# Attention probabilities: two f16 parts turned by one transposing DMA per head, in place of four TensorE transposes

## The chip, the cores and the metric

The kernel runs on one core of one Trainium2 chip. The metric is the device time of one execution in microseconds; lower is better. TensorE (PE), VectorE (DVE), ScalarE (ACT), GpSimd (POOL) and SyncE (SP) each run their own instruction list in order and meet only at semaphores. DMAs are issued by SP here, all on one queue. SBUF and PSUM are the two on-chip memories; TensorE writes only to PSUM.

## What is computed

Two layers over `x` of 32 x 64 x 256: cross-attention and a mixture of experts, then a second attention and a grouped feed-forward. Only the first attention is touched:

```python
q = _proj_heads(input_q, Wq, bq)          # 32 batches, 8 heads, 256 x 8 each
k = _proj_heads(input_k, Wk, bk)
v = _proj_heads(input_v, Wv, bv)
scores = jnp.einsum('bhnd,bhmd->bhnm', q, k) / math.sqrt(D_HEAD)
scores = scores + key_masks[:, None, :, :]
attn = jax.nn.softmax(scores, axis=-1)
out = jnp.einsum('bhnm,bhmd->bhnd', attn, v)
```

For each of 32 x 8 = 256 pairs of batch and head there is a 256 x 256 matrix of probabilities, which must be transposed before it multiplies V, since TensorE contracts over partitions.

## The kernel before

The program is a software pipeline written out by hand. Every engine runs the loop `for n in steps: step(n)`; a step holds eight half steps `i = 0..7`, and half step `g = 8 * n + i` of steps 0 to 31 is batch `n`, head `i`. There are 256 of these. The order of the calls inside `step` is the order on the engine; no scheduler changes it.

For a half step g the chain over the engines is: TensorE `scores(g)` (two matmuls of 256 columns into the PSUM bank `ps1`, shown as `ps` in the profile); VectorE `maxima(g)` (adds the mask, takes the row's extreme into `low_max`, once for each half of the rows); ScalarE `exps(g)` (into `p32`, f32 in SBUF, shown as `p`); TensorE `turn_p(g)` (four 128 x 128 f32 transposes into the PSUM bank `psT`); ScalarE `p_high(g)` (the f16 high part `p_hi`, scaled by 4096); VectorE `p_low(g)` (the f16 rest `p_lo`); TensorE `times_v(g)` (eight matmuls of 25 columns into `psV`). `scores(g)` waits for `exps(g - 1)`, since there is one score bank. Once per step VectorE takes `psV` out with `pv_out`, the only place that runs line 1075.

Three other streams are woven into the same half steps:

- Steps 0 to 7: weights of one expert per step are loaded by SP in three stages of 512 KB, turned by TensorE, copied by ScalarE and split in f16 parts by GpSimd (`w_parts`, lines 486 and 488).
- Steps 5 to 36: 128 units of the experts, one for each two half steps. TensorE `unit_gate` (even half), `unit_up` (odd half), `unit_down` (both); ScalarE `unit_tanh` and `unit_high`; VectorE `gate_mul` (odd half), `up_mul` (even half), `add_expert`; GpSimd `h_low` (line 493).
- For each pair of steps: projections, `cut_qk` and `cut_v` on GpSimd, layer norms and the router (`attention_to_x`, `norm2`, `route_keep`) on VectorE. SP stores the split q and k to DRAM (`store_parts`) and loads them again in stacked form (`load_stacks`, 12 DMAs).

Steps 35 to 43 hold the second layer, which the change does not edit.

## Time and profile before

| | |
|---|---|
| runs | 1111.68, 1112.45, 1113.06 us, median 1112.45 |
| profiled execution | 1112.29 us, of which the span is 1110.4 us |
| PE busy | 921.4 us (83%) |
| DVE busy | 846.0 us (76%) |
| ACT busy | 581.6 us (52%) |
| POOL busy | 364.3 us (33%) |
| DMA queue q1 | 53.93 MB, 16.2% of 16 engines |

The span runs from the first to the last instruction. Busy time is the union of an engine's instructions; instructions of one engine overlap a little, so the start of one and the start of the next say more about its pace than its duration. The 256 half steps lie between about 41 and 867 us.

### The profile page before, as it was taken

What the parts mean: (1) busy time and instruction counts of PE and PEld (TensorE: products, weight loads), DVE (VectorE), ACT (ScalarE), POOL (GpSimd) and SP (SyncE); (2) the same over time, 40 slices, a digit from 0 to 9 for tenths busy, and PEclk for the clock granted to TensorE, in tenths of its full rate; (3) what the DMA queues carried; (4) which work ended last, traced back from release to release, by engine and by line L of the source; (5) the groups of instructions that cost most, each with busy time, mean ns of one, the idle gap of its engine ahead of it and who ended that gap; (6) DMA issues with size and microseconds to landing.
All of it is one profiled execution on the core that took longest, in us unless ns stands there. A gap on an engine that the chain in (4) does not pass through costs nothing.

```text
span 1110.4 us, 26634 instructions
## 1 busy us (share of the span) xinstructions
PE 921.4 (83%) x10039; PEld 813.5 (73%) x10039; DVE 846.0 (76%) x2442; ACT 581.6 (52%) x1258; POOL 364.3 (33%) x410
## 2 busy tenths in 40 slices
PE   2465658889999999999999999999999979866564
PEld 1355547878888888888888888888888857755454
DVE  2556757787989889898989898898988676565552
ACT  1355555566666666666666666666666313322221
POOL 5456454644142322323232323322312322221111
PEclk9867678999999999999999999999999989887877
DMA  4623232302020202111020202011000040001000
GB/s 135 174 68 119 67 119 68 120 31 63 11 63 11 72 2 73 32 43 55 19 63 12 63 12 72 25 44 44 26 12 1 1 143 11 2 25 35 20 30 19
DMA packets 49186, 55.62 MB, mean 50 GB/s; under 512 B 4380, under 2 KB 42276, under 8 KB 49060
## 3 DMA queue, kind: packets, MB, share of 16 engines
q1 hardware_dynamic: 49060, 53.93, 16.2%
q8 instruction: 80, 1.31, 0.5%
q14 instruction: 46, 0.38, 0.1%
HBM read 45.53 MB, written 8.39 MB: 49 GB/s over the span
## 4 chain that ended last, share of the span: by engine, by line
PE 49%; DVE 19%; issue 12%; ACT 10%; POOL 6%; DMA 1%; SPq 1%; DVEq 0%; POOLq 0%; ACTq 0%
PE psG L699 10%; PE psY L699 8%; PE psT L769 8%; PE psU L699 7%; PE ps L699 6%; PE psV L699 4%; ACT p L581 4%; DVE th_ga_h L1143 3%; ACT p_hi L589 2%; DVE ps L1057 2%; PE psM L699 2%; DVE x_res L1162 2%; PE psV L870 1%; POOL hp_lo L493 1%; DVE gt L1132 1%
## 5 line engine op out<-in xcount | busy, mean ns | idle before, releaser
L493 POOL TENSOR_TENSOR hp_lo<-th_ga_h,hp_hi 128x512 f16<-128x512 f32 x128 | 149.5, 1168 | 498.4 <-ACT hp_hi L614 498.4
L1057 DVE CUSTOM_DVE_ANT_0 ps<-ps,mask_in 128x256 f32<-128x256 f32 x512 | 207.3, 446 | 80.0 <-PE ps L699 77.0
L589 ACT ACTIVATE p_hi<-psT 128x512 f16<-128x512 f32 x256 | 152.6, 596 | 213.9 <-PE psT L769 212.5
L581 ACT ACTIVATE p<-ps,low_max 128x256 f32<-128x256 f32 x512 | 214.5, 472 | 77.4 <-DVE low_max L1057 77.3
L1066 DVE SCALAR_TENSOR_TENSOR p_lo<-psT,p_hi 128x512 f16<-128x512 f32 x256 | 176.3, 689 | 36.4 <-ACT p_hi L589 31.2
L699 PE MATMUL psU<-xT,w_gu 128*128 128x256 f16 x1536 | 189.6, 273 | 16.7 <-DVE th_ga_h L1151 10.9
L699 PE MATMUL psG<-xT,w_gu 128*128 128x256 f16 x1536 | 190.6, 274 | 5.4 <-issue 3.5
L699 PE MATMUL psY<-w_dn,hp_hi 128*128 128x256 f16 x1024 | 183.8, 275 | 0.2 <-POOL hp_lo L493 0.2
L699 PEld LDWEIGHTS psU<-xT,w_gu 128*128 128x128 f16 x1536 | 141.7, 98 | 35.3 <-DVE th_ga_h L1151 12.9
L769 PE MATMUL psT<-ident,p 128*128 128x128 f32 x1024 | 164.8, 287 | 0.0
L699 PEld LDWEIGHTS psG<-xT,w_gu 128*128 128x128 f16 x1536 | 142.8, 98 | 22.4 <-issue 6.1
L699 PE MATMUL ps<-k_stack,q_stack 128*128 128x256 bf16 x512 | 104.0, 287 | 62.4 <-ACT p L581 52.7
L699 PE MATMUL psY<-w_dn,hp_lo 128*128 128x256 f16 x512 | 140.7, 275 | 0.0
L769 PEld LDWEIGHTS psT<-ident,p 128*128 128x128 f32 x1024 | 129.6, 149 | 4.2
L699 PEld LDWEIGHTS psY<-w_dn,hp_hi 128*128 128x128 f16 x1024 | 100.9, 99 | 12.6 <-POOL hp_lo L493 0.3
L608 ACT ACTIVATE th_ga_h<-psG 128x512 f32<-128x512 f32 x128 | 76.5, 598 | 61.9 <-PE psG L699 59.3
L699 PEld LDWEIGHTS ps<-k_stack,q_stack 128*128 128x128 bf16 x512 | 42.3, 99 | 83.5 <-ACT p L581 63.1
L1143 DVE SCALAR_TENSOR_TENSOR th_ga_h<-th_ga_h,psG 128x512 f32<-128x512 f32 x128 | 86.7, 677 | 11.7 <-ACT th_ga_h L608 11.3
L699 PEld LDWEIGHTS psV<-v_parts,p_hi 128*128 128x128 f16 x1024 | 77.0, 99 | 21.5 <-issue 17.7
L1151 DVE SCALAR_TENSOR_TENSOR th_ga_h<-psU,th_ga_h 128x512 f32<-128x512 f32 x128 | 86.9, 679 | 3.8 <-PE psU L699 3.8
L699 PE MATMUL psV<-v_parts,p_hi 128*128 128x25 bf16 x1024 | 78.8, 176 | 12.7 <-DVE o_rec L1077 12.7
L614 ACT ACTIVATE hp_hi<-th_ga_h 128x512 f16<-128x512 f32 x128 | 81.0, 633 | 11.9 <-DVE th_ga_h L1151 11.9
(153 smaller groups left out, 1255.8 us busy)
## 6 DMA issues: line engine op xcount, KB each, us to landing
mask_in<-in_mask_Bx2048x_ff SPq DMA_DIRECT2D x32, 256.0 KB, 3.3
part_scratch<-parts SPq DMA_DIRECT2D x16, 384.0 KB, 3.0
q_stack<-part_scratch SPq DMA_DIRECT2D x64, 96.0 KB
k_stack<-part_scratch SPq DMA_DIRECT2D x64, 96.0 KB
stage<-in_L_ffn_gate_w SPq DMA_DIRECT2D x8, 512.0 KB, 4.4
stage<-in_L_ffn_up_w SPq DMA_DIRECT2D x8, 512.0 KB, 5.0
stage<-in_L_ffn_down_w SPq DMA_DIRECT2D x8, 512.0 KB, 4.2
ctx_in<-in_ctx SPq DMA_DIRECT2D x16, 128.0 KB, 3.1
```

Source lines behind the costliest of these rows:

```text
L493: pool.tensor_tensor(hp_lo[:, u % 2, :], hb32[:, u % 2, :], hp_hi[:, u % 2, :], ALU.subtract).then_inc(s["h_split"], 1)
L581: act.activation(p32[:, g % 2, nt, :], ps1[:, nt, :], ACT.Exp, bias=low_max[:, col:col + 1], scale=-1.0).then_inc(s["exp_done"], 1)
L589: act.activation(p_hi[:, g % 2, :, :], psT[:, :].rearrange("p (m n) -> p m n", m=2), ACT.Copy, scale=P_SCALE).then_inc(s["phi_done"], 1)
L608: act.activation(th, psG[:, :], ACT.Tanh, scale=0.5 * G_UNSCALE).then_inc(s["tanh_done"], 1)
L614: act.activation(hp_hi[:, u % 2, :], hb32[:, u % 2, :], ACT.Copy).then_inc(s["h_hi"], 1)
L699: return pe.matmul(out_, lhsT, rhs, start=start, stop=stop, skip_group_check=shares_bank)
L769: last = pe.transpose(psT[:, at:at + P], p32[:, g % 2, nt, mt * P:mt * P + P], ident[:, :])
L1057: dve.tensor_tensor_reduce(out=ps1[:, nt, :], in0=ps1[:, nt, :], in1=mask_in[:, n % 2, nt, :], scale=-1.0, scalar=HIGH, op0=ALU.add, op1=A ...
L1066: dve.scalar_tensor_tensor(out=p_lo[:, g % 2, :, :], in0=psT[:, :].rearrange("p (m n) -> p m n", m=2), scalar=P_SCALE, in1=p_hi[:, g % 2, ...
L1143: dve.scalar_tensor_tensor(out=ga, in0=th, scalar=1.0, in1=psG[:, :], op0=ALU.add, op1=ALU.mult).then_inc(s["gate_used"], 1)
L1151: dve.scalar_tensor_tensor(out=hb32[:, u % 2, :], in0=psU[:, :], scalar=0.5 * G_UNSCALE * G_UNSCALE, in1=ga, op0=ALU.mult, op1=ALU.mult).t ...
L1162: dve.scalar_tensor_tensor(out=x_res[:, row, :], in0=psY[:, eg % 2, t * D:t * D + D], scalar=tokw[:, row * NE + e:row * NE + e + 1], in1=x ...
```

## The change

`turn_p` goes, and with it 1024 TensorE transposes. ScalarE's `p_high` and VectorE's `p_low` now read the exponentials from `p32` in SBUF, before they are turned, and write the two parts side by side into `p_parts`, which has three slots. SP then issues one transposing DMA for each half step (`turn`), from `p_parts` to `p_turn`, 128 rows of 1024 f16 values, that is eight squares of 128 x 128. `times_v` reads `p_turn` and runs one half step later. The factor 4096 moves into the exponent: VectorE adds log 4096 to the two maxima in a new instruction of its own, after `maxima`, and `exps` waits for it. The bank `psT`, now free, becomes the second score bank, so `scores(g)` waits for `exps(g - 2)`.

The units of the experts start two half steps later (`unit_at`), the layer norm and router pieces move by two half steps, `add_expert` stands behind the gate and up products, `pv_out` moves from i = 1 to i = 3, and the two halves of `cut_qk` move one place later, the second one into the next even step. On SP the loads are spread over the half steps between the transposes. `LOW_ON_POOL = 8 * B` is 256, so `p_low` of every half step runs on VectorE and the GpSimd form is never issued.

```diff
+LOW_ON_POOL = 8 * B
-P_SCALE = 4096.0
+LOG_P_SCALE = math.log(4096.0)
...
+        exp_bias = eb("exp_bias", [P, 2, 2], F32)
         p32 = eb("p32", [P, 2, 2, 256], F32)
-        p_hi = eb("p_hi", [P, 2, 2, 256], F16)
-        p_lo = eb("p_lo", [P, 2, 2, 256], F16)
+        p_parts = eb("p_parts", [P, 3, 2, 2, 256], F16)
+        p_turn = eb("p_turn", [P, 3, 2, 2, 2, P], F16)
...
-            u = 4 * (n - FIRST) + hp - lag
+            u = 4 * (n - FIRST) + hp - 1 - lag
...
+        def score_bank(g):
+            return (ps1[:, :, :], psT[:, :].rearrange("p (t m) -> p t m", t=2))[g % 2]
+        def turned(g):
+            return s[f"p_turned{g % 3}"], 16 * (g // 3 + 1)
...
+            def turn(g):
+                sem, count = low_done(g)
+                sp.wait_ge(s["phi_done"], g + 1)
+                sp.wait_ge(sem, count)
+                if g >= 3:
+                    sp.wait_ge(s["pv_done"], g - 2)
+                sem, count = turned(g)
+                sp.dma_start(p_turn[:, g % 3, :, :, :, :].rearrange("p a t m n -> p (a t m) n"),
+                             p_parts[:, g % 3, :, :, :].rearrange("p a t m -> p (a t m)"), transpose=True
+                             ).then_inc(sem, 16)
...
+                for i in range(8):
+                    g = 8 * n + i
+                    if 1 <= g <= 8 * B:
+                        turn(g - 1)
+                    if i == 0 and 1 <= n and n + 1 < B:
+                        sp.wait_ge(s["max_done"], 16 * n)
+                        load_mask(n + 1, (n + 1) % 2)
+                    if even and i == 1 and 1 <= q and q + 1 < NPAIR:
+                        sp.wait_ge(s[f"stack{1 - par}_loaded"], STACK_DMAS * 16 * ((q + 1) // 2))
+                        store_parts(1 - par, q + 1)
...
+                    if even and 3 <= i < 7 and q + 1 < NPAIR:
+                        sp.wait_ge(s["scores_done"], 8 * n)
+                        load_stacks(1 - par, q + 1, i - 3)
+                    if n < NE and i in (2, 4, 6):
+                        load_weight_stage(n + 1, i // 2 - 1)
...
             def exps(g):
-                act.wait_ge(s["max_done"], 2 * g + 2)
+                act.wait_ge(s["bias_done"], g + 1)
                 if g >= 2:
-                    act.wait_ge(s["p_turned"], g - 1)
+                    act.wait_ge(*low_done(g - 2))
...
             def p_high(g):
-                act.wait_ge(s["p_turned"], g + 1)
-                if g >= 2:
-                    act.wait_ge(s["pv_done"], g - 1)
-                act.activation(p_hi[:, g % 2, :, :], psT[:, :].rearrange("p (m n) -> p m n", m=2), ACT.Copy, scale=P_SCALE
-                               ).then_inc(s["phi_done"], 1)
+                act.wait_ge(s["exp_done"], 2 * g + 2)
+                if g >= 3:
+                    act.wait_ge(*turned(g - 3))
+                act.activation(p_parts[:, g % 3, 0, :, :], p32[:, g % 2, :, :], ACT.Copy).then_inc(s["phi_done"], 1)
...
-                if g:
-                    pe.wait_ge(s["exp_done"], 2 * g)
+                if g >= 2:
+                    pe.wait_ge(s["exp_done"], 2 * (g - 1))
...
-            def turn_p(g):
-                pe.wait_ge(s["exp_done"], 2 * g + 2)
-                if g:
-                    pe.wait_ge(s["plo_done"], g)
-                for mt in range(2):
-                    for nt in range(2):
-                        at = mt * 256 + nt * P
-                        last = pe.transpose(psT[:, at:at + P], p32[:, g % 2, nt, mt * P:mt * P + P], ident[:, :])
-                last.then_inc(s["p_turned"], 1)
...
-                pe.wait_ge(s["plo_done"], g + 1)
+                pe.wait_ge(*turned(g))
...
+                dve.wait_ge(s["max_done"], 2 * g + 2)
+                dve.tensor_scalar(exp_bias[:, g % 2, :], low_max[:, 2 * i:2 * i + 2], LOG_P_SCALE, None, ALU.add
+                                  ).then_inc(s["bias_done"], 1)
...
-                if g >= 2:
-                    dve.wait_ge(s["pv_done"], g - 1)
-                dve.scalar_tensor_tensor(out=p_lo[:, g % 2, :, :], in0=psT[:, :].rearrange("p (m n) -> p m n", m=2),
-                                         scalar=P_SCALE, in1=p_hi[:, g % 2, :, :], op0=ALU.mult, op1=ALU.subtract
-                                         ).then_inc(s["plo_done"], 1)
+                if g >= 3:
+                    dve.wait_ge(*turned(g - 3))
+                dve.tensor_tensor(p_parts[:, g % 3, 1, :, :], p32[:, g % 2, :, :], p_parts[:, g % 3, 0, :, :], ALU.subtract
+                                  ).then_inc(s["plo_done"], 1)
```

TensorE in a half step of the middle steps before, from one pair of score matmuls to the next (`psT<-ident,p` are the transposes, `psY` the down product):

```order
L699 MATMUL ps<-k_stack,q_stack 128x256 x2
L769 MATMUL psT<-ident,p 128x128 x4
L699 MATMUL psV<-v_parts,p_hi 128x25 x2
L699 MATMUL psV<-v_parts,p_lo 128x25 x2
L699 MATMUL psV<-v_parts,p_hi 128x25 x2
L699 MATMUL psV<-v_parts,p_lo 128x25 x2
L699 MATMUL psU<-xT,w_gu 128x256 x12
L699 MATMUL psY<-w_dn,hp_hi 128x256 x2
L699 MATMUL psY<-w_dn,hp_lo 128x256
L699 MATMUL psY<-w_dn,hp_hi 128x256 x2
L699 MATMUL psY<-w_dn,hp_lo 128x256
```

TensorE in such a half step of the changed kernel:

```order
L746 MATMUL psT<-k_stack,q_stack 128x256 x2
L746 MATMUL psU<-xT,w_gu 128x256 x12
L746 MATMUL psY<-w_dn,hp_hi 128x256 x2
L746 MATMUL psY<-w_dn,hp_lo 128x256
L746 MATMUL psY<-w_dn,hp_hi 128x256 x2
L746 MATMUL psY<-w_dn,hp_lo 128x256
L746 MATMUL psV<-v_parts,p_turn 128x25 x8
```

The four transposes are gone and the eight matmuls with V stand last. VectorE at the same place (an even half step with `bias_to_v`), before:

```order
L1057 ISA ps,low_max<-ps,mask_in 128x256
L1057 ISA low_max 128x1
L1057 ISA ps,low_max<-ps,mask_in 128x256
L1057 ISA low_max 128x1
L1066 SCALAR_TENSOR_TENSOR p_lo<-psT,p_hi 128x512
L1151 SCALAR_TENSOR_TENSOR th_ga_h<-psU,th_ga_h 128x512
L1046 TENSOR_TENSOR rem<-psM,bias_v 128x2x128
```

VectorE there in the changed kernel:

```order
L1091 ISA ps,low_max<-ps,mask_in 128x256
L1091 ISA low_max 128x1
L1091 ISA ps,low_max<-ps,mask_in 128x256
L1091 ISA low_max 128x1
L1095 TENSOR_SCALAR exp_bias<-low_max 128x2
L1103 TENSOR_TENSOR p_parts<-p,p_parts 128x512
L1187 SCALAR_TENSOR_TENSOR th_ga_h<-psU,th_ga_h 128x512
L1198 SCALAR_TENSOR_TENSOR x_res<-psY,tokw,x_res 128x256
L1080 TENSOR_TENSOR rem<-psM,bias_v 128x2x128
```

One instruction is added (line 1095), and the low part now has both inputs in SBUF (line 1103) where one was in PSUM. SP's queue in an even step of the middle, in the changed kernel:

```order
L386 DMA_TRANSPOSE p_turn<-p_parts 128x8x128
L323 DMA part_scratch<-parts 128x6x256
L386 DMA_TRANSPOSE p_turn<-p_parts 128x8x128
L406 DMA ctx_in<-in_ctx 128x256
L386 DMA_TRANSPOSE p_turn<-p_parts 128x8x128
L333 DMA q_stack<-part_scratch 24x1x2048
L338 DMA k_stack<-part_scratch 24x1x2048
L343 DMA q_stack<-part_scratch 8x2048
L386 DMA_TRANSPOSE p_turn<-p_parts 128x8x128
```

Before, this queue held no transpose; now each one stands behind whatever SP waits for ahead of it, here the store of `parts` and the loads of the stacks.

## Rows read from the trace of the kernel before

**Rows 1.** The page's head and its part 1: busy time of each engine.

```profile
span 1110.4 us, 26634 instructions
PE 921.4 (83%) x10039; PEld 813.5 (73%) x10039; DVE 846.0 (76%) x2442; ACT 581.6 (52%) x1258; POOL 364.3 (33%) x410
```

**Rows 2.** Windows of 50 us: busy by engine, granted clock, DMA share, GB/s.

```profile
100.00:150.00 50.00, 30.63 (x261) 27.08 (x258) 31.86 (x98) 26.93 (x61) 24.91 (x31) 0.66 0.31 91
...
200.00:250.00 50.00, 43.15 (x462) 39.36 (x461) 40.21 (x113) 30.87 (x67) 30.24 (x35) 1.00 0.27 83
...
450.00:500.00 50.00, 47.52 (x527) 42.27 (x525) 44.52 (x134) 31.44 (x69) 15.42 (x17) 1.00 0.14 41
```

**Rows 3.** Timeline of VectorE, line 1075, steps 1, 5, 8, 10, 32: start, us.

```profile
68.75 0.55 DVE L1075 TENSOR_REDUCE o_sum<-psV 128x128 f32<-128x384 f32 x1
...
177.73 0.55 DVE L1075 TENSOR_REDUCE o_sum<-psV 128x128 f32<-128x384 f32 x1
...
267.56 0.55 DVE L1075 TENSOR_REDUCE o_sum<-psV 128x128 f32<-128x384 f32 x1
...
318.00 0.55 DVE L1075 TENSOR_REDUCE o_sum<-psV 128x128 f32<-128x384 f32 x1
...
866.90 0.55 DVE L1075 TENSOR_REDUCE o_sum<-psV 128x128 f32<-128x384 f32 x1
```

**Rows 4.** Timeline of TensorE's weight loads: the transposes and what follows.

```profile
505.12 0.47 PEld L769 LDWEIGHTS psT<-ident,p 128*128 128x128 f32 x4
...
505.56 0.21 PEld L699 LDWEIGHTS psV<-v_parts,p_hi 128*128 128x128 f16 x2
```

**Rows 5.** Timeline of VectorE: end of `maxima`; and a chain of waiting instructions.

```profile
481.27 0.14 DVE L1057 DVE_READ_ACCUMULATOR2_ANT low_max<- 128x1 f32 x1
481.27 0.69 DVE L1066 SCALAR_TENSOR_TENSOR p_lo<-psT,p_hi 128x512 f16<-128x512 f32 x1
...
491.68 0.16 DVE L1114 TENSOR_REDUCE lmax<-lg 128x1 f32<-128x8 f32 x1
491.88 0.15 DVE L1115 TENSOR_SCALAR lmax<-lmax 128x1 f32<-128x1 f32 x1
491.95 0.42 DVE L1057 CUSTOM_DVE_ANT_0 ps<-ps,mask_in 128x256 f32<-128x256 f32 x1
```

**Rows 6.** Groups of VectorE by form: count | busy us, mean ns | idle before.

```profile
L1187 DVE SCALAR_TENSOR_TENSOR d_dn<-d_st,d_dn 128x512 f16<-128x512 f32 x4 | 2.8, 692 | 0.4
...
L1197 DVE TENSOR_SCALAR cve<-cmv 128x2 f32<-128x2 f32 x16 | 2.7, 169 | 0.6
```

**Rows 7.** Single lines of VectorE: duration ns min/median/max, first and last start.

```profile
L1132 DVE TENSOR_TENSOR gt<-gt,probs x16: 224/1172/1209, 129.7 to 888.3; 128x64 f32<-128x64 f32 x16
...
L1038 DVE TENSOR_SCALAR xn<-x_res,mean_var,rstd x16: 403/1398/1403, 12.9 to 740.1; 128x256 f32<-128x256 f32 x16
...
L1093 DVE TENSOR_SCALAR ve<-mv x16: 153/154/154, 101.9 to 871.9; 128x1 f32<-128x1 f32 x16
```

**Rows 8.** Timeline of ScalarE, GpSimd and VectorE around one `h_low`.

```profile
499.89 0.84 ACT L581 ACTIVATE p<-ps,low_max 128x256 f32<-128x256 f32 x2
...
500.62 0.63 ACT L614 ACTIVATE hp_hi<-th_ga_h 128x512 f16<-128x512 f32 x1
...
501.33 1.16 POOL L493 TENSOR_TENSOR hp_lo<-th_ga_h,hp_hi 128x512 f16<-128x512 f32 x1 [5.89 <-ACT hp_hi L614]
...
501.40 1.17 DVE L1132 TENSOR_TENSOR gt<-gt,probs 128x64 f32<-128x64 f32 x1
```

**Rows 9.** The page's parts 3 and 6: the DMA queue; one issue, us to landing.

```profile
q1 hardware_dynamic: 49060, 53.93, 16.2%
...
part_scratch<-parts SPq DMA_DIRECT2D x16, 384.0 KB, 3.0
```

**Rows 10.** Waits: who for whom, total us, times, longest us.

```profile
DVE xn L1098 <- POOL rstd L480: 17.1, 14, 3.7
...
SPq L302 <- POOL parts L425: 373.0, 14, 34.4
```

More of the change, by code:

```diff
@@ L397, in _ @@
             sp.wait_ge(s["dve_step"], 1)
-            load_stacks(0, 0)
+            for piece in range(4):
+                load_stacks(0, 0, piece)
             store_parts(1, 1)
@@ L494, in h_low, with p_low @@
                                    ).then_inc(s["h_split"], 1)
+            def p_low(g):
+                pool.wait_ge(s["phi_done"], g + 1)
+                if g >= 3:
+                    pool.wait_ge(*turned(g - 3))
+                pool.tensor_tensor(p_parts[:, g % 3, 1, :, :], p32[:, g % 2, :, :], p_parts[:, g % 3, 0, :, :],
+                                   ALU.subtract).then_inc(s["plo_pool"], 1)
             def late_pow(j, i):
@@ L509, in step @@
                     u1 = unit_at(n, hp, 1)
+                    if LOW_ON_POOL <= 8 * n + 2 * hp - 1 < 8 * B:
+                        p_low(8 * n + 2 * hp - 1)
                     if (n, hp) == (0, 3):
@@ L523, in step @@
                         w_parts(n, hp, 1)
+                    if LOW_ON_POOL <= 8 * n + 2 * hp < 8 * B:
+                        p_low(8 * n + 2 * hp)
                     if u1 is not None:
@@ L527, in step @@
                         cut_v((q + 1) % 2, q + 1)
-                    if n % 2 == 1 and hp >= 2 and q + 2 < NPAIR:
-                        cut_qk(q + 2, hp == 2)
+                    if n % 2 == 1 and hp == 3 and q + 2 < NPAIR:
+                        cut_qk(q + 2, True)
+                    if n % 2 == 0 and n and hp == 0 and q + 1 < NPAIR:
+                        cut_qk(q + 1, False)
             for n in steps:
@@ L782, in times_v @@
                     dst = psV[:, (nt * H + h) * VC:(nt * H + h + 1) * VC]
-                    for i, (part, mt) in enumerate(((p_hi, 0), (p_hi, 1), (p_lo, 0), (p_lo, 1))):
-                        last = mm(dst, part[:, g % 2, mt, nt * P:nt * P + P], v_parts[:, par, mt, b2 * H + h, :],
+                    for i, (part, mt) in enumerate(((0, 0), (0, 1), (1, 0), (1, 1))):
+                        last = mm(dst, p_turn[:, g % 3, part, nt, mt, :], v_parts[:, par, mt, b2 * H + h, :],
                                   start=(i == 0), stop=(i == 3))
@@ L970, in step @@
                         copies += 1
-                    if 2 <= g <= 8 * B + 1:
-                        times_v(g - 2)
                     u0, u2 = unit_at(n, hp, 0), unit_at(n, hp, 2)
@@ L980, in step @@
                         unit_down(u2, half)
+                    if 3 <= g <= 8 * B + 2:
+                        times_v(g - 3)
                     if (n % 2, i) == (0, 0) and q + 1 < NPAIR:
@@ L983, in step @@
                         project_v((q + 1) % 2, q + 1)
-                    if tail is not None and (n % 2, i) == (0, 2):
+                    if tail is not None and (n % 2, i) == (0, 4):
                         if tail:
@@ L1287, in step @@
                             late_masked(ja)
-                    if done is not None:
-                        add_expert(done, half)
                     if half == 0:
@@ L1297, in step @@
                             gate_mul(u0)
+                    if i == 3 and 1 <= n <= B:
+                        pv_out(n - 1)
+                    if done is not None:
+                        add_expert(done, half)
                     if n == 0 and i < 6:
```

110 lines of the change are left out of this document (49 added, 61 removed).

## The prediction

> **What bounds the kernel now.** I read the page's busy times first [rows 1]: TensorE 83%, VectorE 76%. That is a mean over stages, so next came the starts of line 1075, which VectorE runs once per step [rows 3]. From step 8 to 10 there are 318.00 - 267.56 = 50.44 us, 3.15 us for each half step; over steps 8 to 31 it is (866.90 - 267.56) / 192 = 3.12. Steps 1 to 4 take (177.73 - 68.75) / 32 = 3.41, steps 5 to 7 (267.56 - 177.73) / 24 = 3.74. The 243 us after 866.9 are edited only through the shift of the units.
>
> In a window of the middle [rows 2] TensorE is busy 47.52 of 50 us and VectorE 44.52. So both are nearly full there: 2.81 us of VectorE in each half step of 3.15. What the change can win in the middle is at most VectorE's idle 0.34 us, however much TensorE gives back. From 100 to 150 us no engine is full (VectorE 31.86, TensorE 30.63, GpSimd 24.91, clock at 0.66 of full); there the chain through one score bank sets the pace, and a second bank can pay.
>
> **What is removed.** Four transposes take TensorE's weight loader from 505.12 to 505.56 [rows 4], 0.44 us per half step, 113 us over 256. TensorE then needs about 2.6 us per half step. From 200 to 250 us it is busy only 43.15 of 50 us and its clock is granted in full [rows 2], so I charge nothing for a slower clock.
>
> **What is added on VectorE.** The last accumulator read of `maxima` runs 481.27 to 481.41, and `p_low` starts at 481.27 beside it [rows 5]. The new add must wait for that read; such a wait costs 0.04 us (491.84 to 491.88), and the next free instruction starts 0.07 us after such a small one [rows 5]. So `p_low` starts at 481.52 and not 481.27: +0.25 us per half step. `p_low` itself stays as long: an operation of 512 elements with both inputs in SBUF took 692 ns [rows 6], against 0.69 us from PSUM [rows 5].
>
> **What is added by GpSimd.** Line 1132 (both inputs in SBUF) takes 224 ns at best and 1172 in the median, and line 1038 403 and 1398 [rows 7]; at 501.40 it began beside `h_low` on GpSimd and ended 0.08 us after it [rows 8]. Such instructions wait until GpSimd's current one is over. The page "SBUF — State Buffer" of the Trainium skill (who interferes with whom) has that as a rule: two SBUF inputs, or a two-port mode, contend for one exclusive port pair with GpSimd, where one PSUM input does not. This case's rows agree with it, and by that page alone the old `p_low` was exempt and the new one is not.
>
> Already inside the 2.81 us are about 1.0 + 0.95 us per 16 half steps from these two lines, 0.12 each; without them VectorE needs 2.69, with the add 2.94, with the short gaps in chains 2.97. Now the new part. `h_low` comes after `exps` and `unit_high` of the odd half: `exps` could start 1.10 us into it, `unit_high` 0.73 later, lasting 0.63, then 0.08 [rows 8], so GpSimd is busy from 2.54 to 3.70 us, and what waits is let in near 3.56 (the 224 ns in which line 1132 ended at 502.57). VectorE's odd half lasts 0.73 + 0.25 + 0.60 + 0.60 = 2.18 us plus extras, and its next add stands 0.90 later. Over the eight odd halves of a pair of steps: one without extras waits 0.5, one with the norm 0.2, two with only `add_expert` 0.1, two with `pv_out` 0.6 each (its tensor_scalar), one with `route_keep` 0.6, one nothing: 2.7 / 16 = 0.17. GpSimd's other work (15.42 us busy in 50 less eight `h_low` of 1.16, 12% of the time, some 0.4 us left of each) adds 0.07. VectorE needs 3.21 us. Bounds: 2.97 with no collision; 3.40 if twice as many. Whether the add of two elements collides is open: one element never did (154 ns at most [rows 7]), two were 169 in a stretch where GpSimd hardly works [rows 6]; I count it as colliding, since otherwise `p_low` right behind it does.
>
> **The sum**, on the profiled execution's 1112.3 us:
>
> - Steps 8 to 31: 3.21 against 3.12, 192 half steps: +17 (bounds -29, +54).
> - Steps 1 to 4: VectorE 31.86 / 50 x 3.41 = 2.17, plus 0.25, plus two exposures to a GpSimd that is busy 1.70 us of each half step (58% at the new pace, 0.49 us left on average: 0.28 each): 2.98. I take 2.95: -0.46 x 32 = -15 (bounds -26 at 2.6, +0).
> - Steps 5 to 7: 40.21 / 50 x 3.74 = 3.01, plus 0.25, plus 0.5: 3.76, so 0 (bounds -7, +5). Step 0: -2. That `norm2` waited for GpSimd's power, 17.1 us in all [rows 10], ends by the move of two half steps; it is idle time and inside these.
> - The units end two half steps later, in the stage where TensorE has only them: +3 (0 to 6.3).
> - SP: `store_parts` now stands ahead of transposes and waits for `cut_qk`. SP waited 373.0 us there, 14 times [rows 10], with nothing behind it. The second half of `cut_qk` is over some 5.6 us after half step 1 of an even step begins (3.70 plus GpSimd's cast and subtraction), so that transpose is 1 us late, then runs behind 384 KB, which take 3.0 us [rows 9]. It has about 2.3 half steps, 7 us, before `times_v` asks. +4 (0 to 28, 2 us x 14).
>
> 1112.3 + 17 - 15 - 2 + 3 + 4 = 1119, and the median of the runs stands at the same 1112.4.
>
> **The transposing DMA.** No row shows one. It moves 0.26 MB. From below: q1 took 16.2% of 16 engines for 53.93 MB [rows 9], 3.3 us per MB: 0.87 us. From above: 2878 engine us over 49060 packets are 58.7 ns a packet; in rows of 256 bytes, 1024 packets on 16 engines, 3.76 us. It costs nothing below 3.1 us of queue time and some 7 us of latency. I take the lower side, since the row's bytes are the same and the queue is mostly idle (DMA share 0.14 in the middle [rows 2]). The page "DMA: Bandwidth & Descriptors" of the Trainium skill (latency and other measured facts) gives 261 GB/s for transposing DMAs, by which it would be about 1.0 us plus a fixed 2, an estimate from that page; the page "VectorE: DVE Perf Modes" (the three transpose paths) gives 1309 ns for one square of 128 x 128, by which eight in series would be 10.5 us and the kernel far slower. No run here shows either.
>
> **The rivals.**
>
> - *VectorE's gap is used* (0.35). Collisions fall beside its idle time, and the second bank frees the early steps. 3.0 in the middle (-23), 2.7 in steps 1 to 4 (-23), 3.5 in steps 5 to 7 (-6), with -2, +3, +4: 1065; 1050 to 1105. For it: VectorE waited for scores and for `p_hi` before and no longer does. Against: the alignment above.
> - *The transposing DMA is the bound* (0.18), slower. At 3.76 us instead of (866.90 - 68.75) / 248 = 3.22: +0.54 x 248 = +134, 1246. It decides from 3.2 us each. For it: small pieces; against: the bytes.
> - *SP's waits are the bound* (0.05). `times_v` runs late once per pair: up to +28 on no gain elsewhere, 1140.
>
> **How the numbers follow.** My forecast, VectorE as the only bound at 3.21 us, has 0.42, with a range of its own of 1100 to 1145, of which 0.06 lies on the faster side and 0.07 within 0.2% (2.2 us, about what a measurement of this kernel can tell from no change). Faster: 0.34 of the first rival and 0.06; same: 0.07 and 0.01; slower: 0.29 + 0.18 + 0.05. The range of 8 in 10 reaches from 1070, into the first rival, to 1255, past the second; left out are its lower third and a DMA slower than 3.8 us.
>
> **What would show it.** Right: TensorE idle over 0.4 us per half step in the middle and VectorE over 93% busy there; the new `p_low` at 0.69 us where GpSimd rests, with a second group at 1.0 us or more; half steps of steps 1 to 4 under 3.1 us. The first rival: few long `p_low`, half steps of 3.0. The second: TensorE waiting for the DMA in most half steps, queue share over 0.8. Wrong altogether would be a clock below full in the middle, or a transpose that lands more than 7 us after its issue.

## The result, and the profile after

The changed kernel takes 1128.56 us in the median of 4 runs (1127.45 to 1129.73), the kernel before 1112.76 (4 runs) beside it: a ratio of 1.0127, 95% interval [1.0099, 1.0156]. It is slower by 16 us. I had forecast 1119. Its profiled execution took 1129.38 us.

The page's head and part 1 of the changed kernel, to set beside [rows 1]:

```profile
span 1127.7 us, 25144 instructions
PE 840.7 (75%) x9015; PEld 684.4 (61%) x9015; DVE 913.2 (81%) x2698; ACT 578.3 (51%) x1258; POOL 388.8 (34%) x409
```

TensorE has lost 81 us of work, as the transposes left, and VectorE has gained 67 us. Windows of the changed kernel (columns as in [rows 2]), then those from 300 to 800 us, the first of the kernel before, the second of the changed one:

```profile
100.00:150.00 50.00, 23.24 (x209) 17.77 (x209) 37.69 (x119) 29.25 (x62) 28.41 (x31) 0.57 0.86 175
200.00:250.00 50.00, 39.63 (x412) 33.58 (x412) 43.29 (x120) 29.81 (x63) 32.66 (x34) 0.97 0.70 128
450.00:500.00 50.00, 41.97 (x456) 33.89 (x455) 48.03 (x147) 31.18 (x69) 16.23 (x17) 1.00 0.62 122
```

```profile
300.00:800.00 500.00, 475.47 (x5242) 423.15 (x5241) 444.94 (x1317) 316.03 (x685) 153.87 (x170) 1.00 0.14 41
```

```profile
300.00:800.00 500.00, 420.83 (x4488) 339.54 (x4486) 470.78 (x1438) 301.60 (x668) 162.02 (x168) 0.99 0.62 121
```

In the middle one engine is nearly full now and no longer two: VectorE 48.03 of 50 us, TensorE 41.97. The timeline of the line that VectorE runs once per step (1111 now, 1075 in [rows 3]), at steps 1, 5, 8, 10 and 32:

```profile
73.64 0.55 DVE L1111 TENSOR_REDUCE o_sum<-psV 128x128 f32<-128x384 f32 x1
...
176.09 0.55 DVE L1111 TENSOR_REDUCE o_sum<-psV 128x128 f32<-128x384 f32 x1
...
266.16 0.55 DVE L1111 TENSOR_REDUCE o_sum<-psV 128x128 f32<-128x384 f32 x1
...
318.15 0.55 DVE L1111 TENSOR_REDUCE o_sum<-psV 128x128 f32<-128x384 f32 x1
...
879.26 0.55 DVE L1111 TENSOR_REDUCE o_sum<-psV 128x128 f32<-128x384 f32 x1
```

These starts, with [rows 3], give the pace of the stages. But this mark stands two half steps later in its step than before, so the first and the last stage can't be compared by it. `maxima` has kept its place. Its first instruction starts at 63.04 us before and 62.94 after in step 1, at 170.53 and 164.37 in step 5, at 261.74 and 254.47 in step 8, and at 860.64 and 869.44 in the last half step of step 31. The column "in all" goes by these starts:

| stage | before, by the mark | after, by the mark | in all, us | forecast |
|---|---|---|---|---|
| to step 1, us | 68.75 | 73.64 | 0 | -2 |
| steps 1 to 4, us a half step | 3.41 | 3.20 | -6 | -15 |
| steps 5 to 7 | 3.74 | 3.75 | -1 | 0 |
| steps 8 to 31 | 3.12 | 3.19 | +16 | +17 |
| from there to the end, us | 243.5 | 248.4 | +8 | +3, and +4 for SP |

So the forecast had the middle nearly right, too much gain in steps 1 to 4, and too little loss at the end.

How far one profiled execution can be trusted is seen where kernels run the same code. In steps 1 to 4 three of the kernels below (act_add, act_low64, act_low64_cut) do, and their half steps take 3.11, 3.16 and 3.27 us; three others (changed, low64, cut_later) take 3.20, 3.20 and 3.19. In the middle, two such pairs agree within 0.01 us.

**Where VectorE's time went in the middle.** From 300 to 800 us, groups of VectorE in the kernel before (count | busy us, mean ns | idle before):

```profile
L1066 DVE SCALAR_TENSOR_TENSOR p_lo<-psT,p_hi 128x512 f16<-128x512 f32 x159 | 109.4, 688 | 15.2 <-ACT p_hi L589 11.3
...
L1038 DVE TENSOR_SCALAR xn<-x_res,mean_var,rstd 128x256 f32<-128x256 f32 x9 | 12.6, 1399 | 0.0
L1132 DVE TENSOR_TENSOR gt<-gt,probs 128x64 f32<-128x64 f32 x10 | 11.7, 1173 | 0.3
```

and in the changed kernel:

```profile
L1103 DVE TENSOR_TENSOR p_parts<-p,p_parts 128x512 f16<-128x512 f32 x155 | 112.2, 724 | 0.3 <-issue 0.3
...
L1095 DVE TENSOR_SCALAR exp_bias<-low_max 128x2 f32<-128x2 f32 x155 | 40.1, 258 | 5.3
...
L1116 DVE TENSOR_SCALAR o_rec<-o_rec,gates 128x16 f32<-128x16 f32 x19 | 14.2, 746 | 0.7
```

The sum of maxima and logarithm costs 258 + 34 ns (5.3 us of gaps over 155) in each half step, `p_low` only 36 ns more than before. Of the 155 sums 128 took at most 0.25 us; the 27 longer ones each overlap a `h_low`. The 155 `p_low` have 11 long ones, 10 of them beside the subtraction of `cut_v` on GpSimd. The line of `o_rec` now collides with GpSimd; the two long lines of before came to stand elsewhere and fell to 408 and 226 ns. That the sum collides, and with what, is seen in two timelines of the changed kernel, VectorE's and then GpSimd's (`hp_lo` is `h_low`):

```profile
479.34 0.17 DVE L1095 TENSOR_SCALAR exp_bias<-low_max 128x2 f32<-128x2 f32 x1
479.42 0.69 DVE L1103 TENSOR_TENSOR p_parts<-p,p_parts 128x512 f16<-128x512 f32 x1
...
482.72 0.95 DVE L1095 TENSOR_SCALAR exp_bias<-low_max 128x2 f32<-128x2 f32 x1
483.58 0.68 DVE L1103 TENSOR_TENSOR p_parts<-p,p_parts 128x512 f16<-128x512 f32 x1
```

```profile
482.49 1.15 POOL L528 TENSOR_TENSOR hp_lo<-th_ga_h,hp_hi 128x512 f16<-128x512 f32 x1
```

`h_low` ends at 483.64. The sum, begun at 482.72, ends at 483.67: 0.95 us for four bytes twice in each row. Where GpSimd rests it takes 0.17. Whoever comes next after such a sum finds GpSimd's instruction over, which is why `p_low` is seldom long.

**Where the early gain went.** Waits from 74 to 176 us (steps 1 to 4), who for whom, total us, times, longest us; in the kernel before:

```profile
PE ps L699 <- ACT p L581: 30.4, 26, 2.1
```

and in the changed kernel:

```profile
PE psV L746 <- DMA p_turn<-p_parts: 36.3, 16, 6.1
```

The second bank took away TensorE's wait for the exps, 30.4 us, and a wait for the turned parts, 36.3 us, took its place. VectorE was busy only 76.82 of these 102 us, so it did not set the pace here. Over the same stretch the granted clock was 0.71 before and 0.58 after, with TensorE busy 62.5 and 53.5 of 102 us.

The chain of work in the changed kernel, from 152.9 us on (start, us, what), shows one way in which the turned parts are late. SPq is the queue that issues DMAs; L386 is the transposing one, L333, L338, L343 and L346 reload the stacks, L315 loads weights:

```profile
152.91 0.34 SPq L386
...
153.35 0.70 SPq L333
...
154.10 0.64 SPq L338
...
154.79 0.46 SPq L346
...
155.30 0.41 SPq L315
...
155.82 1.27 SPq L386
...
157.19 0.70 SPq L333
...
157.94 0.64 SPq L338
...
158.64 0.46 SPq L343
...
159.22 1.27 SPq L386
...
163.21 4.73 DMA p_turn<-p_parts
```

For ten microseconds the chain is SP's issuing, one issue behind the other: 3.40 us from one transposing DMA to the next (155.82 to 159.22), and 3.99 to the one after that (163.21), where a weight load stands between as well. That last one lands 4.73 us after its issue begins. The transposing DMAs themselves, in the changed kernel, the page's parts 3 and 6, beside [rows 9]:

```profile
q1 hardware_dynamic: 319396, 121.07, 52.6%
...
p_turn<-p_parts SPq DMA_TRANSPOSE x256, 3.2
```

The view of the tile `p_turn`, first from 74 to 176 us, then from 300 to 800 (SP's issue in ns, min/median/max; the last row of each is from issue to landing):

```profile
L386 SPq DMA_TRANSPOSE p_turn<-p_parts x33: 1231/1238/2468, 74.2 to 175.6; - x33
...
DMA to landing us min/median/max: 3.0/4.1/7.0
```

```profile
L386 SPq DMA_TRANSPOSE p_turn<-p_parts x156: 1231/1235/2528, 299.2 to 799.8; - x156
...
DMA to landing us min/median/max: 3.0/3.2/4.8
```

In the middle 256 KB land in 3.2 us and nearly nothing waits for them. By the DMA share of the two windows from 300 to 800, one costs 0.62 x 3.19 - 0.14 x 3.12 = 1.5 us of all 16 engines; my bounds were 0.87 and 3.76. Its rival, the DMA as the bound, needed 3.2 and fell.

### The profile page after: what moved, and what is told of

It reads as the page before. It is cut to its first block, busy times and chain, and to the rows that moved or that the text cites. A ratio compares the mean times of both kernels' runs of the same rounds, so it can differ in the third digit from the quotient of the medians.

```text
span 1127.7 us, 25144 instructions
## 1 busy us (share of the span) xinstructions
PE 840.7 (75%) x9015; PEld 684.4 (61%) x9015; DVE 913.2 (81%) x2698; ACT 578.3 (51%) x1258; POOL 388.8 (34%) x409
## 4 chain that ended last, share of the span: by engine, by line
DVE 42%; PE 25%; issue 14%; DMA 5%; ACT 5%; POOL 4%; SPq 3%; DVEq 0%; POOLq 0%; ACTq 0%
DVE psT L1091 5%; PE psG L746 5%; DVE th_ga_h L1187 5%; PE psU L746 5%; DVE ps L1091 5%; DVE th_ga_h L1179 5%; PE psY L746 4%; DMA p_turn<-p_parts 4%; DVE p_parts L1103 3%; PE psV L746 3%; PE ps L746 3%; DVE x_res L1198 2%; PE psT L746 2%; DVE low_max L1091 2%; DVE o_rec L1116 2%
## 5 line engine op out<-in xcount | busy, mean ns | idle before, releaser
L629 ACT ACTIVATE p<-ps,exp_bias 128x256 f32<-128x256 f32 x256 | 107.5, 471 | 160.1 <-DVE exp_bias L1095 159.8
L1103 DVE TENSOR_TENSOR p_parts<-p,p_parts 128x512 f16<-128x512 f32 x256 | 182.9, 715 | 0.7 <-ACT p_parts L637 0.3
L746 PE MATMUL psV<-v_parts,p_turn 128*128 128x25 bf16 x2048 | 92.1, 176 | 112.1 <-DVE o_rec L1113 58.2
L746 PEld LDWEIGHTS psV<-v_parts,p_turn 128*128 128x128 f16 x2048 | 87.0, 98 | 134.9 <-issue 65.9
L637 ACT ACTIVATE p_parts<-p 128x512 f16<-128x512 f32 x256 | 161.7, 632 | 9.4 <-DMA p_turn<-p_parts 8.2
L629 ACT ACTIVATE p<-psT,exp_bias 128x256 f32<-128x256 f32 x256 | 107.5, 471 | 110.1 <-DVE exp_bias L1095 108.8
L1091 DVE CUSTOM_DVE_ANT_0 ps<-ps,mask_in 128x256 f32<-128x256 f32 x256 | 103.5, 446 | 34.3 <-PE ps L746 33.0
L1091 DVE CUSTOM_DVE_ANT_0 psT<-psT,mask_in 128x256 f32<-128x256 f32 x256 | 103.3, 444 | 26.0 <-PE psT L746 25.3
L1095 DVE TENSOR_SCALAR exp_bias<-low_max 128x2 f32<-128x2 f32 x256 | 70.1, 274 | 8.8
L1091 DVE DVE_READ_ACCUMULATOR2_ANT low_max<- 128x1 f32 x512 | 72.0, 141 | 0.0
```

The costliest lines, as they stand in the source:

```text
L629: act.activation(p32[:, g % 2, nt, :], score_bank(g)[:, nt, :], ACT.Exp, bias=exp_bias[:, g % 2, nt:nt + 1], scale=-1.0).then_inc(s["exp_d ...
L637: act.activation(p_parts[:, g % 3, 0, :, :], p32[:, g % 2, :, :], ACT.Copy).then_inc(s["phi_done"], 1)
L746: return pe.matmul(out_, lhsT, rhs, start=start, stop=stop, skip_group_check=shares_bank)
L1091: dve.tensor_tensor_reduce(out=score_bank(g)[:, nt, :], in0=score_bank(g)[:, nt, :], in1=mask_in[:, n % 2, nt, :], scale=-1.0, scalar=HIGH ...
L1095: dve.tensor_scalar(exp_bias[:, g % 2, :], low_max[:, 2 * i:2 * i + 2], LOG_P_SCALE, None, ALU.add).then_inc(s["bias_done"], 1)
L1103: dve.tensor_tensor(p_parts[:, g % 3, 1, :, :], p32[:, g % 2, :, :], p_parts[:, g % 3, 0, :, :], ALU.subtract).then_inc(s["plo_done"], 1)
```

## The experiments

Twelve kernels, each timed beside the kernel before on its own chip; each is the changed kernel with an edit, of which the main lines are shown. For those that bear on the middle, from its profiled execution: the half step of steps 8 to 31, and what VectorE was busy and idle in it (its busy time from 300 to 800 us over 500, times the half step).

| kernel | us, ratio to before | half step 8 to 31 | busy | idle |
|---|---|---|---|---|
| before | | 3.122 | 2.78 | 0.34 |
| changed | 1128.56, 1.0127 | 3.193 | 3.01 | 0.19 |
| no_add | 1096.72, 0.9849 | 3.040 | 2.80 | 0.24 |
| add_unused | 1123.62, 1.0091 | 3.164 | 3.00 | 0.16 |
| act_add | 1116.78, 1.0010 | 3.130 | 2.89 | 0.24 |
| hlow8 | 1101.66, 0.9895 | 3.078 | 2.91 | 0.17 |
| no_add_hlow8 | 1069.35, 0.9598 | 2.929 | 2.68 | 0.25 |
| low64 | 1124.26, 1.0093 | 3.166 | 2.67 | 0.49 |
| act_low64 | 1080.70, 0.9694 | 2.964 | 2.08 | 0.89 |

### What the sum costs: no_add, add_unused, act_add

**no_add.** No sum; the exps take the maxima as bias, and 4096 comes in at the cast and in the subtraction (`p_low` becomes a scalar_tensor_tensor, 689 ns in the median against 692).

```diff
-                act.wait_ge(s["bias_done"], g + 1)
+                act.wait_ge(s["max_done"], 2 * g + 2)
...
-                dve.wait_ge(s["max_done"], 2 * g + 2)
-                dve.tensor_scalar(exp_bias[:, g % 2, :], low_max[:, 2 * i:2 * i + 2], LOG_P_SCALE, None, ALU.add
-                                  ).then_inc(s["bias_done"], 1)
```

> The changed kernel without the instruction on line 1095: the factor 4096 goes back into the high part's copy on ScalarE and into the low part on VectorE, both read from SBUF. Theory A (VectorE is the bound in the middle; the add costs 0.25 us of it, plus its collisions with GpSimd, mean 274 ns against 170): a half step of steps 8 to 31 falls from 3.19 to about 2.90 us, 192 x 0.29 = 56 us, and little changes in steps 0 to 4; about 1075 us. Theory B (the transposing DMA and SP's queue set the pace everywhere): no change beyond 5 us, about 1125.

Measured: 1096.72 us, ratio 0.9849 [0.983, 0.9869]. Without this one small instruction the change is faster than the kernel before: it costs 32 us, more than the whole loss. That is less than I had expected: the half step fell to 3.04 us and not to 2.90. VectorE's idle time went up by 0.05 us, and `p_low` grew longer, as the lines under act_add show.

**add_unused.** The sum stays with its wait, but nothing reads it; the exps and 4096 are as in no_add.

```diff
-                act.wait_ge(s["bias_done"], g + 1)
+                act.wait_ge(s["max_done"], 2 * g + 2)
```

> VectorE still makes the sum of each half step's two maxima and the logarithm, at the same place and after the same wait, but nothing reads it: the exps take the maxima themselves as their bias, and the factor 4096 comes in at the cast and in the subtraction for the low part. So VectorE's occupancy stays and the step from the maxima to the exps is gone. The kernel without the sum was 1094.8 us in its profiled execution, the changed one 1127.7: 32.9 us. If the whole cost of the sum is VectorE's occupied time (my step in the prediction), this kernel stays at the changed kernel's time, about 1128 us, with 3.19 us a half step in the middle. If the whole cost is the way from the maxima to the exps, it comes to about 1097 us and 3.04 us. The kernel with the sum on ScalarE, which frees VectorE but keeps a step on the way, ended between (1116.8 us), so I expect both to count, about 1112 us and 3.12 us in the middle.

Measured: 1123.62 us, 1.0091 [1.0067, 1.0115]; 3.164 us a half step. I had expected a cost from both sides in equal parts; taking the sum off the way to the exps, with VectorE still making it, is worth 5 of the 32 us, and VectorE is as busy as in the changed kernel.

**act_add.** The sum on ScalarE, which waits for the maxima and then makes it.

```diff
+                act.activation(exp_bias[:, g % 2, :], low_max[:, at:at + 2], ACT.Copy, bias=LOG_P_SCALE
+                               ).then_inc(s["bias_done"], 1)
...
-                dve.tensor_scalar(exp_bias[:, g % 2, :], low_max[:, 2 * i:2 * i + 2], LOG_P_SCALE, None, ALU.add
-                                  ).then_inc(s["bias_done"], 1)
```

> The changed kernel with the addition of log 4096 moved from VectorE to ScalarE, ahead of exps; the low part stays the plain subtraction. Theory A: VectorE's time is what counts, so the middle half step falls to 3.04 us as without the instruction, and ScalarE (61% busy) takes the 0.2 us unnoticed: about 1097. A rival: the latency between maxima and exps is what the instruction costs, then ScalarE's version, with the same latency, stays near 3.15 to 3.19 and 1120 to 1128.

Measured: 1116.78 us (10 runs), 1.001 [0.9992, 1.0028], no difference from before. Its profiled execution, at 1110.44, was the fastest of the ten, so the row of the table flatters it a little. The group of `p_low` from 300 to 800 us tells where part of the freed time went, first in no_add, then in act_add:

```profile
L1100 DVE SCALAR_TENSOR_TENSOR p_parts<-p,p_parts 128x512 f16<-128x512 f32 x164 | 130.4, 795 | 2.0 <-ACT p_parts L637 2.0
```

```profile
L1104 DVE TENSOR_TENSOR p_parts<-p,p_parts 128x512 f16<-128x512 f32 x158 | 132.9, 841 | 3.6 <-ACT p_parts L641 3.1
```

Without the sum ahead of it `p_low` itself meets `h_low`: 795 and 841 ns in the mean, where it was 724. Of the sum's 0.29 us the row of VectorE gets back 0.21 in no_add, 0.12 in act_add. Those over 0.8 us, 45 in no_add and 46 in act_add, all overlap a `h_low`. The three kernels together: off the way alone gives 5 us, off VectorE alone 12, and both 32; so the two do not add. The time on VectorE is worth 12 us taken first and 27 taken last, the way to the exps 5 first and 20 last. VectorE's time is thus the larger part in either order, and the step to the exps counts once VectorE has room. (act_add's step also occupies ScalarE, which no run separates from the delay.)

### Collisions with GpSimd: hlow8, no_add_hlow8, low64

**hlow8.** `h_low` on 8 of 128 columns of each tile; the rest of h's low part stays zero.

```diff
-                pool.tensor_tensor(hp_lo[:, u % 2, :], hb32[:, u % 2, :], hp_hi[:, u % 2, :], ALU.subtract
+                pool.tensor_tensor(hp_lo[:, u % 2, 0:8], hb32[:, u % 2, 0:8], hp_hi[:, u % 2, 0:8], ALU.subtract
```

> The changed kernel with h_low on GpSimd cut from 512 to 8 columns, the rest of the low part of h being zero; everything else waits as before. Theory A with collisions as the second cost: the long add instructions and long low parts of steps 8 to 31 mostly vanish, half step 3.19 to about 3.03, so -30 us or so there; the last stage may gain some us as well. About 1095. If collisions cost nothing because VectorE had slack there: within 5 us of 1128.

Measured: 1101.66 us, 0.9895 [0.9871, 0.9918]. 27 us go with `h_low`'s length. In the middle the gain is 3.193 - 3.078 = 0.115 us a half step, where I had counted 0.17 for the new collisions with `h_low`. VectorE's busy time falls by 0.10 of it. Groups of VectorE in hlow8, 300 to 800 us:

```profile
L1106 DVE TENSOR_TENSOR p_parts<-p,p_parts 128x512 f16<-128x512 f32 x160 | 110.4, 690 | 0.3 <-issue 0.3
...
L1098 DVE TENSOR_SCALAR exp_bias<-low_max 128x2 f32<-128x2 f32 x160 | 47.0, 294 | 5.5
...
L1119 DVE TENSOR_SCALAR o_rec<-o_rec,gates 128x16 f32<-128x16 f32 x20 | 4.7, 234 | 0.7
```

The expectation that the long sums vanish did not come true: the sum went from 258 to 294 ns in the mean, as its 26 long ones now overlap the instructions of `cut_qk` and `cut_v` on GpSimd. What grew shorter is `o_rec` (746 to 234 ns), the router's `keep` (770 to 232) and `p_low` (724 to 690): 0.06, 0.03 and 0.04 us a half step. So the run shows what VectorE pays for all collisions with `h_low`, and not what the sum's own cost.

**no_add_hlow8.** Both edits.

> No sum on VectorE, and h's low part on GpSimd only 8 of 128 columns wide (the rest of it stays zero). Each alone gave 3.04 and 3.08 us a half step in the middle, against 3.19 of the changed kernel. If VectorE is the bound of the middle and both only take from its row of work (the sum 0.15, the collisions with h's low part 0.115), they add: 2.93 us a half step there, and 47 half steps by another 0.11 below the kernel without the sum: about 1090 us. If the two are the same loss seen twice (the sum delays the exps, and so puts h's low part on top of VectorE's copies), the second gives nothing more: about 1097 us. If TensorE, with about 2.9 us of work a half step, becomes the bound in their place, the time ends near 1085 to 1090 us as well, and the row of waits tells it: VectorE then waits for TensorE.

Measured: 1069.35 us, 0.9598 [0.9576, 0.962]; 2.929 us a half step, where 3.193 - 0.153 - 0.115 = 2.925 was the sum of the two. They add fully in the middle: two separate costs in one engine's row of work. The time that I had expected, 1090, counted 47 half steps at the lower pace where the middle has 192.

**low64.** From step 8 on (half step 64), `p_low` runs on GpSimd.

```diff
-LOW_ON_POOL = 8 * B
+LOW_ON_POOL = 64
```

> The changed kernel with the low parts of half steps 64 to 255 on GpSimd (the constant that the change itself has). Theory A: VectorE loses 0.60 us per half step from step 8 on and gets more collisions (GpSimd busy 70%); TensorE with about 2.65 us is the next bound. Half step near 2.85: 192 x 0.34 = 65 us, about 1063. Theory B: no change. A third way: GpSimd, in order, delays h_low and with it unit_down, and the half step stays above 3.1.

Measured: 1124.26 us, 1.0093 [1.007, 1.0117]. VectorE loses 0.34 us of work a half step, and the half step only 0.03, not the 0.34 expected. The sum still stands on VectorE and now meets a GpSimd that is busy 330.75 of 500 us: its median is 404 ns there where it was 170. It stands ahead of the exps. That this is what keeps the half step long is shown only by act_low64 below.

### The early steps: plain_copy, w_on_act, w_small

**plain_copy.** The same bytes by an ordinary DMA; the parts arrive unturned.

```diff
-                sp.dma_start(p_turn[:, g % 3, :, :, :, :].rearrange("p a t m n -> p (a t m) n"),
-                             p_parts[:, g % 3, :, :, :].rearrange("p a t m -> p (a t m)"), transpose=True
+                sp.dma_start(p_turn[:, g % 3, :, :, :, :].rearrange("p a t m n -> p (a t m n)"),
+                             p_parts[:, g % 3, :, :, :].rearrange("p a t m -> p (a t m)")
```

> The changed kernel with a plain SBUF to SBUF copy of the same 256 KB in place of the transposing DMA; the parts are not turned, so the attention's result is another one. Theory A: in steps 1 to 4, where TensorE waited 36 us for the transposing DMA beside the weight loads, half steps fall from 3.20 to near 2.9 us, 10 us in all; steps 8 to 31 stay at 3.19 within 0.03. About 1118. Theory B: the middle falls too, to 3.0 or less, below 1090.

Measured: 1120.47 us, 1.0063 [1.004, 1.0086]. In its view of the tile `p_turn` from 300 to 800 us:

```profile
L386 SPq DMA_DIRECT2D p_turn<-p_parts x156: 464/465/539, 301.0 to 796.9; - x156
...
DMA to landing us min/median/max: 2.2/2.3/5.1
```

The turning itself thus costs 0.77 us of SP's issue and 0.9 us of landing, and 8 us in all. In the middle the half step goes from 3.193 to 3.174, in steps 1 to 4 from 3.20 to 3.13, not to the 2.9 expected; the latter is no more than the same code differs by from one profiled execution to the next.

**w_on_act.** The weight loads are issued by ScalarE, not by SP.

```diff
-                    if n < NE and i in (2, 4, 6):
-                        load_weight_stage(n + 1, i // 2 - 1)
...
+                act.dma_start(dst, src).then_inc(s[f"stage{m}_loaded"], 16)
```

> The changed kernel with the 512 KB weight loads of steps 0 to 7 issued from ScalarE's queue, no longer ahead of the transposing DMAs on SP's. Theory C (early steps are held by transposing DMAs that stand behind loads on one queue, up to 6.6 us to landing): half steps of steps 1 to 4 fall from 3.20 to 3.0 or less, 6 to 10 us, 1119 to 1122. If GpSimd's and VectorE's collisions hold them (busy 31 and 38 of 50 us), within 3 us of the changed kernel.

Measured: 1132.34 us, 1.0157 [1.0131, 1.0184]; steps 1 to 4 at 3.36 us a half step, slower than 3.20. The order in SP's queue is not repaired that way. ScalarE is on the way to every transposing DMA, and now waits and issues too, so this run does not clear SP.

**w_small.** The weights of experts 1 to 7 arrive in part.

```diff
+                if e:
+                    dst, src = dst[:, :, 0:64], src[:, :, 0:64]
```

> In the stage in which the experts' weights are loaded (steps 0 to 7) the loads of experts 1 to 7 bring 64 columns of each weight tile only, so far fewer bytes go over the DMA engines there; the weights of these experts are not the reference's. Theory: in steps 1 to 4 the transposing DMAs wait beside the weight loads (the share of the DMA engines is 0.86 to 0.94 there, and TensorE waits for the turned parts, 53.8 us in all), and this is where the gain of the second bank of scores went. Then a half step of steps 1 to 4 falls from 3.20 to 2.95 us or less, that of steps 5 to 7 from 3.75 to under 3.5, and the whole by 8 to 15 us, to about 1115 us; the wait of TensorE for the turned parts nearly goes. Rival: the casts of the weights on GpSimd and VectorE, with the low parts, hold these steps, not the bytes; then steps 1 to 4 stay at 3.1 to 3.2 us (the smaller casts of this kernel, if they shrink, would show as less busy time of these two engines), and the whole falls by less than 4 us.

Measured: 1125.08 us, 1.0102 [1.0071, 1.0133]. The DMA share in steps 1 to 4 falls from 0.92 to 0.71, and the landing is back at 3.2 us:

```profile
L388 SPq DMA_TRANSPOSE p_turn<-p_parts x33: 1231/1246/2376, 75.3 to 174.5; - x33
...
DMA to landing us min/median/max: 3.0/3.2/4.9
```

Yet a half step falls only from 3.20 to 3.12, those of steps 5 to 7 from 3.75 to 3.74, and TensorE still waits 31.0 us for the turned parts in steps 1 to 4. My theory that the weights' bytes hold the early steps fell: they are at most some 0.08 us of it, again no more than such executions differ by.

### The end, and better kernels: cut_later, act_low64, act_low64_cut

**cut_later.** The split of the second layer's weights into f16 parts on VectorE (`late_cut`), four pieces that stand between the last units, each comes two half steps later.

```diff
-CUT_STEP = {TAIL_STEP: {3: 0}, TAIL_STEP + 1: {0: 1, 1: 2, 2: 3}}
+CUT_STEP = {TAIL_STEP + 1: {0: 0, 1: 1, 2: 2, 3: 3}}
```

> The changed kernel with the splits of the last weights (late_cut) moved one place on, from half step 6 of step 33 to steps 34's half steps 0, 2, 4, 6. Theory: of the last stage's 10 us of loss, part is VectorE standing 7.9 us between the router's end at 902.05 and the first weights at 909.95 with no unit in between, where before two units' work stood between them; TensorE's longest wait there was 10.4 us against 6.3. Expected 4 to 7 us less, 1122 to 1124. If the loss is only the two half steps by which the units start later, no change.

Measured: 1126.67 us, 1.0107 [1.0084, 1.013], not told apart from the changed kernel. After the mark of step 32 it takes 246.1 us and not 248.4; nine kernels here that leave both the split and `h_low` alone lie between 247.0 and 249.2.

**act_low64.** The edits of act_add and of low64 together.

> As act_add, and the low parts of half steps 64 to 255 on GpSimd. With both on VectorE gone it is busy about 2.3 us of a half step. With the low part alone moved, the half step was 3.17 and TensorE waited for h_low and VectorE's add took 356 ns in the median; if those collisions were what kept it, the half step now falls below 2.95 (192 x 0.2 = 40 us against the low part alone moved, 1080 or less). If GpSimd's own order is the bound (1.16 us for each low part, 1.16 for each h_low, the cuts), it stays above 3.05.

Measured: 1080.70 us, 0.9694 [0.9664, 0.9723]. Its window from 300 to 800 us:

```profile
300.00:800.00 500.00, 440.06 (x4820) 373.25 (x4818) 350.08 (x1213) 356.51 (x881) 345.98 (x339) 0.98 0.68 129
```

Neither edit alone gave more than 12 us, both give 48. Each alone took away one of VectorE's two partners of GpSimd and left the other: with only the sum gone `p_low` met `h_low` (841 ns), with only `p_low` gone the sum met both (median 404 ns). With both gone nothing that VectorE does between the scores and the exps meets GpSimd: its maxima take 448 ns in the mean, as before (446). VectorE then waits for TensorE's scores, 127.5 of the 500 us, and no engine is over 88% busy.

**act_low64_cut.** act_low64 with the edit of cut_later.

> The best of the kernels so far (the sum on ScalarE, all low parts of the middle on GpSimd: 1080.7 us), with the cut of the experts' units one step later, which alone took 1 to 2 us off the changed kernel. If that gain came from the tail, it stands here too, about 1078.5 us. If it was only noise of the middle, the time is 1080.7 again.

Measured: 1075.40 us, 0.9646 [0.9618, 0.9675], the fastest kernel here that computes everything. The middle is the same (2.959 us); after the mark of step 32 it takes 243.9 us and act_low64 249.1. The longest wait of TensorE for VectorE there, in act_low64 and then in act_low64_cut:

```profile
PE psU L750 <- DVE th_ga_h L1188: 18.9, 8, 11.1
```

```profile
PE psU L750 <- DVE th_ga_h L1188: 15.0, 8, 7.1
```

## Why the prediction was right, and where its terms were off

The sign, and VectorE as what bounds the middle, were right. The total lies 10 us above the forecast: 9 us of early gain that did not come and 5 more at the end, less 4 that SP's wait did not cost; the other terms are off by 1 or 2 us each. Taken by the prediction's own steps:

- **Steps 8 to 31, +17 forecast, +16 measured.** "VectorE needs 3.21 us"; the half step took 3.19. That it agrees to 0.02 us is in part luck: VectorE was busy 3.01 us of it and idle 0.19, where my sum filled the 3.21 with work and all but closed the gaps. The work was counted too high and the idle time too low by about as much. Among the terms, the added 0.25 us of the sum measured 0.29 with its collisions. What was wrong in the step is who collides: I let `p_low` wait for `h_low`, and left it open whether a sum of two elements does. It does, in 27 of 155, and no `p_low` of the middle was long beside `h_low` alone. no_add (-32 us) and no_add_hlow8 (fully additive) show that both costs are mainly VectorE's; by add_unused the delay of the exps is worth 5 us while VectorE is full, and by act_add against no_add up to 20 once it is not. The test I had set for the collisions, "a second group at 1.0 us or more" among the `p_low`, was met in 11 of 155 (mean 724, longest 1207 ns).
- **Steps 1 to 4, -15 forecast, -6 measured.** I had VectorE full there at 2.95 us a half step; it was busy 75% of 3.20. The step that failed is the one that gave the transposing DMA no cost there: "It costs nothing below 3.1 us of queue time and some 7 us of latency". That figure was argued from the middle. In the early steps it lands after 4.1 us in the median (7.0 at most), each occupies SP for 1.24 us, and TensorE waits 36.3 us for the result. So no transpose went past the 7 us of the quoted limit, and the engine waited all the same: the step left out that the issue itself occupies SP, and that each landing stands behind what SP issues ahead of it. Three runs each took one piece: without the transposition a half step was 0.07 us shorter, with fewer bytes of weights 0.08, and with the weight loads issued by ScalarE 0.16 longer. The same code differs by up to 0.15 us between profiled executions, so none of the three is a price. No run took 0.25 at once, and which part holds these steps stays open. The chain row of ten microseconds of SP's issues speaks for the issue time as a large part in even steps, 3.40 us where the half step takes 3.20; that is read from the trace and not isolated by a run. So is the lower clock (0.58 against 0.71), which stretches what TensorE does between these waits: the transposes of gate weights took 339 ns each there before and 408 after.
- **Steps 5 to 7, 0 forecast, -1 measured**, and step 0, -2 forecast and 0 measured.
- **The end, +3 forecast, about +8 measured.** I priced the units' shift at +3, with bounds of 0 and 6.3 us. What I left out is that VectorE, with the units still to come, stands in its order before loads of the last stage. In the timelines of VectorE it waits 2.08 us there before and 4.37 after:

```profile
893.31 0.15 DVE L1278 TENSOR_SCALAR dy_gate<-gates 128x1 f32<-128x1 f32 x1 [2.08 <-DMA m_u<-in_mask_BxS_bk]
```

```profile
906.59 0.15 DVE L1314 TENSOR_SCALAR dy_gate<-gates 128x1 f32<-128x1 f32 x1 [4.37 <-DMA m_u<-in_mask_BxS_bk]
```

  TensorE's longest wait for a unit's product went from 6.3 to 10.4 us. cut_later and act_low64_cut move the split; VectorE's wait at that line is 2.17 us in both, and their ends are 2.3 and 5.2 us shorter. hlow8's end is 5.4 us shorter, though its wait at that line is 5.03 us; so `h_low`, for which the down product waits, bears on the end too, and that wait does not decide it alone. Whether the two overlap was not tried, and how the 5 us above the forecast divide is open.
- **SP's wait for `cut_qk`, +4 forecast.** The wait, 373.0 us in [rows 10], is 41.5 us now, 14 times, with 3.7 us at the longest, and the turned parts are waited for in the middle for 1.2 us in all. It costs nothing that shows there, and the rival that made it the bound fell. In the total this +4 stood in for most of what the end's term lacked, which is luck too.
- **The rival "VectorE's gap is used"**, 1065 us, had the right potential and a wrong premise. VectorE's idle 0.34 us went down to 0.19 and was not won but filled with the sum. no_add_hlow8 comes near its time, at 1069.35 us, but not by its stages: steps 1 to 4 take 3.20 us there and not 2.7, and the middle's 2.93 needs `h_low` cut short.

Of the rule that I set against `p_low`, the page "SBUF — State Buffer" of the Trainium skill (who interferes with whom), the trace agrees with the mechanism: an operation of VectorE with two SBUF inputs that meets GpSimd's gets under way when GpSimd's ends. In no_add the 26 `p_low` that overlap only a `h_low` end 0.55 us after it, and the long sum above ends 0.03 us after it. The rule also holds for the sum, which has one SBUF input (0.95 us against 0.17); the page's other case is a two-port mode, and that the sum runs in one is not shown by a row. By the page "VectorE: DVE Perf Modes" of the Trainium skill (the three transpose paths), eight squares in series would take 10.5 us, an estimate from that page; the trace shows 3.2 for all eight, so they do not run in series at that price.

## What to carry to other kernels

An engine that is nearly full pays for a small new instruction, and again for what it collides with: here two elements per row took 0.29 us of VectorE's time, 0.09 of it by collisions, and leaving them out gave 0.15 us a half step and 32 us in all. The factor that they carry could be had for nothing in instructions that were there. Price an instruction by the wait behind it and by what GpSimd does at that time, not by its size. Two edits that took work off the same full engine gave 12 and 4 us alone and 48 together, so a half that gives little alone does not condemn the pair. And where a wait is taken away from a chain, look at the longest latency left in it: here the wait for the exps (30.4 us) came back as a wait for a DMA (36.3 us).
